# Two attention layers with feed-forwards on one core: biases in a held column of the tokens, parts straight from PSUM, exponentials by head

## The chip, the cores and the metric

One core of a Trainium2 chip. The metric is the device time of one execution in microseconds (us). The kernel before takes 317.99 us (median of three runs, 317.55 to 318.81).

## What is computed

The input is 2048 tokens of 256 channels (two sequences of 1024) and a context of 77 tokens of 192 channels per sequence. Four residual steps follow one another; the tokens are normalised ahead of each:

```
x = x + attention16(layernorm(x), context) # 16 heads of 16 channels, softmax over 77 keys
x = x + y, y = layernorm(n + relu(n @ w1 + b1) @ w2 + b2) * gamma + beta, n = layernorm(x)
x = x + attention1(layernorm(layernorm(x)), layernorm(context)) # one head of 256 channels
x = x + layernorm(x) @ W[e(t)].T + b[e(t)] # e(t): one of 8 matrices, by the position t alone
```

`e(t)` is the argmax over 8 of the product of a fixed position table with the signs of a small matrix. All data is float32. The operands of the products for q, the scores, w1 and w2 are split into a high part (rounded to the engine's fast float32 form, `F32R`) and a low part (the rest), and three products are added: high x high, high x low, low x high.

## The kernel before, in words

The tokens are cut into NG = 8 groups of 256, in two batches of four groups. A group is two halves `i` of 128 tokens, one token per partition. Each group goes through four stages, named by letters: A (first attention), B (feed-forward; Y is the normalisation of its output), C (second attention), D (the routed product). All five engines run their own list of steps, written out by hand at the end of `tensor`, `vector`, `scalar`, `gpsimd` and `sync`. Each engine works through its list strictly in order, waits on semaphores inside the steps, and so interleaves groups and stages as the lists say. Nothing else sets the order.

The steps that the text speaks of, for group g:

- `stats(K, g)` on VectorE: L598, L601, L604, mean and variance. `rs(K, g)` on GpSimd (L1220): the variance to the power of -0.5. `apply(K, g)`: a 2-element product on VectorE (L609, minus mean times that power), then half 0 of the tokens is normalised on VectorE (L619) and half 1 on ScalarE (L1029).
- `tA`, `tB`, `tC`, `tD` on TensorE (L327): transposes into a PSUM bank. `hi` on ScalarE (L1037) copies the bank as the high part XTH; `lo` on VectorE (L625) subtracts and leaves the low part XTL.
- `q(g)`: 12 matmuls (L256); `qh` on ScalarE (L1046) and `ql` on VectorE (L632) add b_q and split, in two instructions each.
- A tile of scores is (g, i, a), a the half of the heads: 32 tiles of 128 tokens x 8 heads x 77 keys. `sc` (L365) writes it into one of the two score banks S. `smax` (L649) takes the maximum by head. For a = 0 it is negated (L652), and ScalarE takes eight exponentials by head with accumulated sums (L1060). For a = 1 VectorE subtracts the maxima into SBUF (L654), one exponential runs over the whole tile (L1064), and VectorE sums (L662). The function `by_head` says which.
- `tE` transposes the exponentials (L375, L377), `rr` and `et` on ScalarE bring reciprocal sums and exponentials into place (L1072, L1083, L1084), `pv`, `o`, `wo`, `x1` finish the attention.
- `w1(g, j)`, j = 0..3: 24 matmuls in pairs of 12, into a bank. `hf` on ScalarE (L1094, two instructions) adds b1, takes the ReLU and writes HF (three buffers). `hh` on VectorE (L682), or `hhA` on ScalarE for j = 1 (L1102), rounds to the high part HH. The low part HL comes from `hlP` on GpSimd (L1254), or `hlD` on VectorE for j = 1, 3 of groups 0, 6, 7 (L688). `w2(g, i, h)`: 12 matmuls, h the half of the hidden channels. `b2` and `be` on GpSimd add bias and beta; `y`, `x2` on VectorE end the stage.
- `r_expert`, `r_position`, `r_index`, `r_pairs` on VectorE: the routing (L837 is an instruction of `r_position`), once. `f_*`: the constants of the second attention, once (L249, L471).
- `pc` on ScalarE (L1139), `pr` on TensorE (L460), `pa` on VectorE (L752): the routed product, eight pairs of 128-token pieces for each batch. Where a piece starts is read from EV by `value_load` the first time. `put` on GpSimd (L1282) stores.

A PSUM bank is held until a step has read it:

```
P = hold(("sc", g, i, a), ("S", k), ("ex", n + 1) if by_head(i, a) else ("sub", n // 2 + 1))
P = hold(("w1", g, j), ("B", p), ("hf", 4 * g + j + 1))
```

Of the kernel before, what the change touches and what calls it, by code (L numbers as in the profile page):

```python
# [15 lines left out]
NK = 77  # L16
CW = 124
NP = 15
# [31 lines left out]
def f(ap):  # L50
    return ap.bitcast(F32)
# [10 lines left out]
def by_head(i, a):  # L62
    return a == 0


def late(g):
    return g in (0, 6, 7)


def hl_on_dve(g, j):  # L70
    return late(g) and j in (1, 3)


def hh_on_act(j):
    return j == 1


def upto(rule, *at):

    g, j = at  # L80
    return sum(bool(rule(a, b)) for a in range(g + 1) for b in range(4) if (a, b) <= (g, j))


def program(nc, A, out):
    with ExitStack() as ctx:
# [12 lines left out]
        nhalf = sb("nhalf", [128, 2])  # L98
        X = sb("X", [128, NG, 2, 256])
# [5 lines left out]
        cols = sb("cols", [128, 22])  # L105
        COLS = dict(b_q=0, b_k=2, bk1=4, bq1=6, bv1=8, g1=10, be1=12, b1=14)
# [18 lines left out]
        HF = sb("HF", [128, 3, 2, 256])  # L125
# [3 lines left out]
        SM = sb("SM", [128, 11, 2, 11])  # L129
# [47 lines left out]

        def raw(n, parts=128, w=512):
            return RAW[0:parts, n % 2, 0:w]
# [40 lines left out]
        def hl_here(w, g, j):  # L220
            if hl_on_dve(g, j):
                w.wait_ge(s["hlD"], upto(hl_on_dve, g, j))
            else:
                w.wait_ge(s["hlP"], 4 * g + j + 1 - upto(hl_on_dve, g, j))

        def hh_here(w, g, j):
            if hh_on_act(j):
                w.wait_ge(s["hhA"], g + 1)
            else:
                w.wait_ge(s["hh"], 3 * g + (j + 1 if j < 1 else j))  # L230

# [3 lines left out]
        def tensor(e):  # L235
# [42 lines left out]
            def vrep(b, p):  # L278
# [3 lines left out]
                w.wait_ge(s["d"], 6)  # L282
# [35 lines left out]
            def turn(K, g, p, signal, until):  # L318
# [4 lines left out]
                w.wait_ge(s["bi" + K], g + 1)  # L323
                P = hold(("t" + K, g), ("B", p), until)
# [87 lines left out]
            def w2(g, i, h, p):  # L412
# [996 lines left out]
```

## Time and profile before

| | |
|---|---|
| median of 3 runs | 317.99 us (317.55 to 318.81) |
| the profiled execution, first to last instruction | 314.0 us |
| its own time beside the span | not listed apart; the median stands 4.0 us over the span |
| mean granted TensorE clock | 0.93 of full speed |
| busy: TensorE matmuls, VectorE | 267.9 us, 254.8 us |
| busy: ScalarE, GpSimd | 181.7 us, 157.3 us |
| DMA moved | 15.3 MB, mean 49 GB/s |

Busy time is the time in which an engine has an instruction under way. The matmuls are pipelined, so a busy TensorE need not be at its peak. Instructions of one engine overlap a little, so the distance between their starts can be less than the duration of one.

### The profile page before, as it was taken

How to read it: one execution, taken by the hardware profiler on the slowest of the kernel's cores; microseconds unless marked ns; L12 is line 12 of the kernel's file. 1: busy time of each engine (PE TensorE's matmuls, PEld its weight loads, DVE VectorE, ACT ScalarE, POOL GpSimd, SP SyncE). 2: the span in 40 equal slices, each digit the busy share in tenths (PEclk: the TensorE clock that was granted, in tenths of full speed). 3: DMA queues.
4: the chain of work that ended last, by engine and by line, in shares of the span. 5: the costliest groups of instructions: out<-in, count | busy, mean ns of one | idle time of the engine just before them, and what ended most of it. 6: DMA issues, size and time to landing. Idle time of an engine off the chain costs nothing.

```text
span 314.0 us, 6283 instructions
## 1 busy us (share of the span) xinstructions
PE 267.9 (85%) x2080; PEld 232.0 (74%) x2080; DVE 254.8 (81%) x664; ACT 181.7 (58%) x606; POOL 157.3 (50%) x157
## 2 busy tenths in 40 slices
PE   2954958977999998999999989999989999878960
PEld 2743937763999698689789959988878988666850
DVE  2998998972889999998997789899899986875640
ACT  2468628526368857478695857775754471454510
POOL 2253640275225878821652263268766653164854
PEclk9995596995999999999999999999999999997995
DMA  6922010240000372100001000011110000000222
GB/s 177 336 72 77 8 42 25 67 142 27 3 0 3 115 222 51 29 24 2 2 0 35 2 0 2 33 52 51 37 36 0 2 0 1 3 0 34 87 78 73
DMA packets 8797, 15.32 MB, mean 49 GB/s; under 512 B 1270, under 2 KB 6813, under 8 KB 8509
## 3 DMA queue, kind: packets, MB, share of 16 engines
q1 hardware_dynamic: 6845, 9.68, 9.2%
q0 software_dynamic: 1920, 5.25, 5.9%
q8 instruction: 17, 0.28, 0.4%
q14 instruction: 15, 0.12, 0.1%
HBM read 11.77 MB, written 3.15 MB: 48 GB/s over the span
## 4 chain that ended last, share of the span: by engine, by line
PE 37%; DVE 29%; issue 15%; POOL 12%; ACT 3%; DVEq 1%; DMA 1%; POOLq 0%; SPq 0%; ACTq 0%
PE PB L256 16%; PE PB L249 7%; PE PB L460 5%; DVE SM L598 3%; POOL SM L1220 3%; DVE SX L649 3%; DVE SM L609 3%; PE S L365 3%; PE S L377 2%; POOL out_x L1282 2%; DVE WD L837 2%; PE PB L327 2%; POOL RAW L1275 2%; DVE XN L701 2%; POOL HL L1254 2%
## 5 line engine op out<-in xcount | busy, mean ns | idle before, releaser
L1220 POOL TENSOR_TENSOR SM<-SM,nhalf 128x2 f32<-128x2 f32 x40 | 29.4, 737 | 98.4 <-DVE SM L604 97.9
L1060 ACT ACTIVATE E<-S,SX 128x77 f32<-128x77 f32 x128 | 39.5, 340 | 16.8 <-DVE SX L652 16.6
L256 PE MATMUL PB<-XTH,W1H 128*128 128x256 f32 x128 | 38.3, 299 | 3.9 <-issue 2.2
L1254 POOL TENSOR_TENSOR HL<-HF,HH 128x512 fp32r<-128x512 f32 x26 | 34.5, 1335 | 13.6 <-DVE HH L682 12.0
L1094 ACT ACTIVATE HF<-PB,cols 128x256 f32<-128x256 f32 x64 | 26.8, 473 | 20.9 <-PE PB L256 20.6
L256 PE MATMUL PB<-W2H,HH 128*128 128x256 f32 x128 | 37.9, 296 | 1.1 <-DVE HL L688 1.1
L256 PE MATMUL PB<-XTH,W1L 128*128 128x256 f32 x128 | 36.4, 284 | 0.0
L256 PE MATMUL PB<-XTL,W1H 128*128 128x256 f32 x128 | 36.4, 284 | 0.0
L256 PE MATMUL PB<-W2H,HL 128*128 128x256 f32 x128 | 35.8, 280 | 0.0
L256 PE MATMUL PB<-W2L,HH 128*128 128x256 f32 x128 | 35.8, 279 | 0.0
L460 PE MATMUL PB<-WD,XP 128*128 x120 | 29.9, 402 | 0.8 <-issue 0.8
L256 PEld LDWEIGHTS PB<-XTH,W1H 128*128 128x128 f32 x128 | 24.5, 192 | 6.2 <-issue 3.9
L649 DVE TENSOR_REDUCE SX<-S 128x8 f32<-128x616 f32 x32 | 25.2, 788 | 3.9 <-PE S L365 3.8
L1060 ACT ACTIVATION_READ_ACCUMULATOR E<-S,SX 128x1 f32 x128 | 28.4, 222 | 0.0
L460 PEld LDWEIGHTS PB<-WD,XP 128*128 128x128 f32 x120 | 23.1, 200 | 5.7 <-issue 2.1
L327 PE MATMUL PB<-ident,XN 128*128 128x128 f32 x128 | 20.1, 289 | 8.0 <-ACT XN L1029 4.7
L1029 ACT ACTIVATE XN<-X,SM 128x256 f32<-128x256 f32 x32 | 19.0, 601 | 13.2 <-DVE SM L609 12.9
L256 PEld LDWEIGHTS PB<-W2H,HH 128*128 128x128 f32 x128 | 24.2, 189 | 2.7 <-issue 2.6
L752 DVE SCALAR_TENSOR_TENSOR X<-PB,MK,X 128x256 f32 x30 | 14.5, 483 | 13.6 <-DVE X L752 6.8
L598 DVE BATCH_NORM_STATS2 SM<-X 128x6 f32<-128x256 f32 x64 | 23.9, 415 | 1.7 <-DMA X<-in_x 1.5
L256 PEld LDWEIGHTS PB<-XTH,W1L 128*128 128x128 f32 x128 | 24.7, 193 | 0.0
L256 PEld LDWEIGHTS PB<-XTL,W1H 128*128 128x128 f32 x128 | 24.6, 192 | 0.0
(188 smaller groups left out, 778.3 us busy)
## 6 DMA issues: line engine op xcount, KB each, us to landing
RAW<-in_w SPq DMA_DIRECT2D x4, 512.0 KB, 5.0
WD<-in_WD SPq DMA_DIRECT2D x2, 1024.0 KB
X<-in_x SPq DMA_DIRECT2D x4, 256.0 KB, 7.1
x<-X SPq DMA_DIRECT2D x4, 256.0 KB, 2.2
bc<-in_rows SPq DMA_DIRECT2D x1, 768.0 KB, 7.3
RAW<-in_w_q SPq DMA_DIRECT2D x1, 256.0 KB, 4.2
Wo<-in_w_o SPq DMA_DIRECT2D x1, 256.0 KB, 7.8
RAW<-in_WqT SPq DMA_DIRECT2D x1, 256.0 KB
```

Of the source, the lines that this page charges most:

```text
L249: t = e.matmul(dst, a, b, start=j == 0, stop=j == len(pairs) - 1)
L256: t = e.matmul(dst, a, b, start=first and j == 0, stop=last and j == n - 1)
L327: t = e.transpose(P[:, c * 256 + i * 128:c * 256 + (i + 1) * 128], xn[:, i, c * 128:(c + 1) * 128], ident[:, :])
L460: t = e.matmul(P[:, v * 256:(v + 1) * 256], XP[:, r % 2, v, c * 128:(c + 1) * 128], WD[:, c, bass.ds(start[n], 256)], start=c == 0, stop=c ...
L598: step(e.bn_stats(smi(K, g, i, 0, 6), src[:, i, :]))
L649: step(e.tensor_reduce(mx_, sv, AX, ALU.max))
L752: t = e.scalar_tensor_tensor(out=x, in0=P[:, v * 256:(v + 1) * 256], scalar=MK[:, n:n + 1], in1=x, op0=ALU.mult, op1=ALU.add)
L1029: e.activation(dst_of(K, g)[:, 1, :], src_of(K, g)[:, 1, :], ACT.Identity, bias=smi(K, g, 1, 10, 11), scale=smi(K, g, 1, 9, 10)).then_inc( ...
L1060: t = e.activation(Ei[:, h * NK:(h + 1) * NK], P[:, at:at + NK], ACT.Exp, bias=SX[:, i, 2, k:k + 1], accum_out=SX[:, i, 1, k:k + 1])
L1094: t = e.activation(HF[:, n % 3, v, :], P[:, v * 256:(v + 1) * 256], ACT.Relu, bias=col("b1", 2 * j + v))
L1220: e.tensor_tensor(sm(K, g, 9), sm(K, g, 8), nhalf[:, :], ALU.pow).then_inc(s["rs" + K], 1)
L1254: e.tensor_tensor(HL[:, hs, :], HF[:, (4 * g + j) % 3, :, :], f(HH[:, hs, :]), ALU.subtract).then_inc(s["hlP"], 1)
```

## The change

- b_q and b1 become the last row of w_q and w1. The normalised tokens of a group sum to zero over the channels, so channel 255 is given by the others: the step `pivot` on VectorE subtracts the last row of the weights from all others, and column 255 of the normalised tokens is held at one. GpSimd's `one` writes it, `apply` leaves it out for A and B, and GpSimd puts the true value back before the residual (in `b2`). The old last rows are loaded, broadcast to 128 partitions, as WQR and W1R.
- With no bias left, `qh` and `ql` are one instruction each, and the high part HH of the feed-forward is a ReLU straight from PSUM on ScalarE (`hh`). The low part is one VectorE instruction from PSUM (`hl`). HF, `hf`, `hhA`, `hlP` and `hlD` are gone; `w2` waits for the two j of its own half. The bank of w1 is held until `hl`.
- All 32 tiles of exponentials are taken by head with sums. The maximum is negated in its own instruction (`negate=True`).
- The product of minus mean and the power moves from VectorE to GpSimd as two 2-element products.
- The routing's values are loaded in one block per engine (`starts`), early.
- All five lists are in a new order.

```
-                P = hold(("w1", g, j), ("B", p), ("hf", 4 * g + j + 1))
+                P = hold(("w1", g, j), ("B", p), ("hl", 4 * g + j + 1))
...
-                for j in range(4):
-                    hh_here(w, g, j)
-                    hl_here(w, g, j)
+                w.wait_ge(s["hh"], 4 * g + 2 * h + 2)
+                w.wait_ge(s["hl"], 4 * g + 2 * h + 2)
...
+            def starts():
+                w.wait_ge(s["route2"], 1)
+                load_starts(e, 0, 7 * 256, start)
...
+            def pivot(n):
+                w.wait_ge(s["m_id"], 1)
+                if n == 0:
+                    step(e.tensor_scalar(nkeep[:, :], ident[:, 127:128].to_broadcast([128, 2]), 1.0, None, ALU.subtract))
+                    settle()
+                w.wait_ge(s[("wq", "w1a", "w1b")[n]], 16)
+                w.wait_ge(s[("wqr", "w1r", "w1r")[n]], 16)
+                W, R, by = ((RAW[:, 0, 0:512], WQR, None), (RAW[:, 1, 0:1024], W1R, -1.0), (RAW[:, 0, 0:1024], W1R, keep))[n]
+                if n == 0:
+                    step(e.scalar_tensor_tensor(out=W[:, 0:256], in0=R, scalar=-1.0, in1=W[:, 0:256], op0=ALU.mult, op1=ALU.add))
+                    W, by = W[:, 256:512], keep
+                e.scalar_tensor_tensor(out=W, in0=R, scalar=by, in1=W, op0=ALU.mult, op1=ALU.add).then_inc(s["wfix"], 1)
...
+                e.tensor_reduce(two(SX[:, i, 0, 8 * a:8 * a + 8]), sv, AX, ALU.max, negate=True).then_inc(s["mx"], 1)
...
+            def hl(g, j):
+                w.wait_ge(s["hh"], 4 * g + j + 1)
                 hs = slice(2 * j, 2 * j + 2)
-                e.tensor_tensor(HL[:, hs, :], HF[:, (4 * g + j) % 3, :, :], f(HH[:, hs, :]),
-                                ALU.subtract).then_inc(s["hlD"], 1)
+                e.scalar_tensor_tensor(out=HL[:, hs, :], in0=two(bank("w1", g, j)[:, :]), scalar=0.0, in1=f(HH[:, hs, :]),
+                                       op0=ALU.max, op1=ALU.subtract).then_inc(s["hl"], 1)
...
+                for h in range(8):
+                    at = h // 4 * 512 + h % 4 * NK
+                    k = 8 * a + h
+                    t = e.activation(E[:, i, a, h * NK:(h + 1) * NK], P[:, at:at + NK], ACT.Exp,
+                                     bias=SX[:, i, 0, k:k + 1], accum_out=SX[:, i, 1, k:k + 1])
                 t.then_inc(s["ex"], 1)
...
+                e.activation(HH[:, 2 * j:2 * j + 2, :], two(bank("w1", g, j)[:, :]), ACT.Relu).then_inc(s["hh"], 1)
...
+                if K != "Y":
+                    e.tensor_tensor(sm(K, g, 11), sm(K, g, 6), minus[:, :], ALU.mult).then_inc(s["nm"], 1)
...
+                    e.tensor_tensor(sm(K, g, 10), sm(K, g, 11), sm(K, g, 9), ALU.mult).then_inc(s["mr" + K], 1)
+                if K == "B":
+                    e.tensor_tensor(sm(K, g, 8), X[:, g, :, LAST], sm(K, g, 9), ALU.mult).then_inc(s["xm"], 1)
```

What stands ahead of w1(0, 0) on TensorE before (PB are banks; WD and RAW rows are the second attention's constants and the routing's permutation):

```order
L375 MATMUL S<-ident,RR 128x128
L377 MATMUL S<-ident,E 124x128 x5
L249 MATMUL PB<-WD,RAW 128x154 x4
L315 MATMUL PB<-WD 128x16 x8
L249 MATMUL PB<-WD,RAW 128x154 x4
L327 MATMUL PB<-ident,XN 128x128 x4
L365 MATMUL S<-KBH,XTH 128x308 x2
...
L256 MATMUL PB<-XTH,W1H 128x256
```

And in the changed kernel (L359 is tE, L371 pv, L347 sc, L309 a transpose, L227 wo):

```order
L371 MATMUL PB<-ET,VB 32x256 x8
L206 TENSOR_LOAD EV
L206 ISA x30
L309 MATMUL PB<-ident,XN 128x128 x4
L227 MATMUL PB<-Wo,RT 128x256 x4
L347 MATMUL S<-KBH,XTH 128x308 x2
L347 MATMUL S<-KBL,XTH 128x308 x2
L347 MATMUL S<-KBH,XTL 128x308 x2
...
L309 MATMUL PB<-ident,XN 128x128 x4
L234 MATMUL PB<-XTH,W1H 128x256
```

The constants are gone from this place. The block of register loads stands ahead of tB(0), and the scores of group 2 and the transpose of group 4 ahead of w1.

ScalarE around the high part of B(0) before (L1083 and L1084 are et, L1037 the high part, L1094 hf):

```order
L1144 ACTIVATE WD<-PB 96x308
L1064 ACTIVATE E<-E 128x616
L1083 ACTIVATE RT<-S 128x128
L1084 ACTIVATE ET<-S 124x5x128
L1029 ACTIVATE XN<-X,SM 128x256
L1072 ACTIVATE RR<-SX 128x128
L1037 ACTIVATE XTH<-PB 128x512
```

And in the changed kernel (L1013 is the high part, L1030 the exponentials, L1058 hh):

```order
L1050 ACTIVATE RT<-S 128x128
L1051 ACTIVATE ET<-S 124x5x128
L206 TENSOR_LOAD EV
L206 ISA x30
L1030 ACTIVATE E,SX<-S,SX 128x77 x16
L1013 ACTIVATE XTH<-PB 128x512
L1005 ACTIVATE XN<-X,SM 128x255
...
L1030 ACTIVATE E,SX<-S,SX 128x77 x8
L1058 ACTIVATE HH<-PB 128x512 x2
```

The block and two tiles of group 2 by head now stand ahead of the high part of B(0).

VectorE at the first routed additions before (L750 are the loads and their checks, L752 the additions):

```order
L750 TENSOR_LOAD EV
L750 ISA x2
L752 ISA
L752 SCALAR_TENSOR_TENSOR X<-PB,MK,X 128x256
...
L598 BN_STATS SM<-X 128x6 x2
L601 BN_AGGR SM<-SM 128x2 x2
L604 TENSOR_SCALAR SM<-SM 128x2
```

And in the changed kernel (L724 the additions, L671 and L677 are x2 of group 7):

```order
L671 SCALAR_TENSOR_TENSOR XN<-XN,SM,bc 128x256 x2
L677 SCALAR_TENSOR_TENSOR X<-XN,SM,X 128x256 x2
L612 TENSOR_SCALAR XN<-X,SM 128x256
L724 ISA
L724 SCALAR_TENSOR_TENSOR X<-PB,MK,X 128x256
```

The additions have no load ahead of them, and the first of them stands behind x2 of the last group, where before two pairs stood ahead of y(7).

## Rows read from the trace of the kernel before

**Rows 1.** The page, part 1: busy time, share of the span, instructions.
```profile
PE 267.9 (85%) x2080; PEld 232.0 (74%) x2080; DVE 254.8 (81%) x664; ACT 181.7 (58%) x606; POOL 157.3 (50%) x157
```

**Rows 2.** Windows: stretch, length, busy of each engine, clock, DMA share, GB/s.
```profile
0.00:83.00 83.00, 58.59 (x437) 48.58 (x438) 62.68 (x174) 43.71 (x148) 32.01 (x38) 0.81 0.29 92
83.00:266.00 183.00, 175.92 (x1488) 156.61 (x1488) 165.79 (x419) 121.94 (x416) 101.85 (x95) 1.00 0.10 30
266.00:304.00 38.00, 33.40 (x159) 26.77 (x157) 25.84 (x71) 16.03 (x42) 18.58 (x19) 0.96 0.10 36
```

**Rows 3.** Waits of TensorE from 0 to 83 us: total, times, longest.
```profile
PE PB L249 <- DMA WKV<-in_w_k: 5.9, 1, 5.9
PE S L365 <- DVE E L654: 4.5, 1, 4.5
```

**Rows 4.** Groups of VectorE: count, busy us, mean ns, idle before.
```profile
L609 DVE SCALAR_TENSOR_TENSOR SM<-SM 128x2 f32<-128x2 f32 x32 | 15.1, 472 | 2.8 <-POOL SM L1220 2.7
L654 DVE TENSOR_TENSOR E<-S,SX 128x616 f32<-128x616 f32 x16 | 12.8, 799 | 0.6
L682 DVE CAST HH<-HF 128x512 fp32r<-128x512 f32 x24 | 12.5, 524 | 8.2 <-ACT HF L1094 7.3 <-issue 0.7
L662 DVE TENSOR_REDUCE SX<-E 128x8 f32<-128x616 f32 x16 | 12.4, 778 | 0.5 <-ACT E L1064 0.5
L625 DVE TENSOR_TENSOR XTL<-PB,XTH 128x512 fp32r<-128x512 f32 x16 | 10.8, 681 | 2.1 <-ACT XTH L1037 1.9
L688 DVE TENSOR_TENSOR HL<-HF,HH 128x512 fp32r<-128x512 f32 x6 | 7.1, 1200 | 0.1
L652 DVE TENSOR_SCALAR SX<-SX 128x8 f32<-128x8 f32 x16 | 5.7, 353 | 0.5
```

**Rows 5.** Groups of GpSimd, same columns.
```profile
L1254 POOL TENSOR_TENSOR HL<-HF,HH 128x512 fp32r<-128x512 f32 x26 | 34.5, 1335 | 13.6 <-DVE HH L682 12.0 <-ACT HH L1102 1.5
L1220 POOL TENSOR_TENSOR SM<-SM,nhalf 128x2 f32<-128x2 f32 x40 | 29.4, 737 | 98.4 <-DVE SM L604 97.9
L1209 POOL TENSOR_TENSOR W1L<-RAW,W1H 128x1024 fp32r<-128x1024 f32 x2 | 4.8, 2390 | 1.2 <-ACT W1H L1003 1.2
```

**Rows 6.** Timeline of VectorE at 18 and 36 us: start, duration.
```profile
17.98 2.00 DVE L609 SCALAR_TENSOR_TENSOR SM<-SM 128x2 f32<-128x2 f32 x1
36.38 6.24 DVE L837 TENSOR_TENSOR WD<-WD 128x64 f32<-128x64 f32 x1
```

**Rows 7.** Timeline of ScalarE: the first of eight heads, and what follows the eighth.
```profile
21.25 0.33 ACT L1060 ACTIVATE E<-S,SX 128x77 f32<-128x77 f32 x1 [3.05 <-DVE SX L652]
...
23.66 0.63 ACT L1029 ACTIVATE XN<-X,SM 128x256 f32<-128x256 f32 x1
```

**Rows 8.** Groups of ScalarE, columns as in rows 4.
```profile
L1094 ACT ACTIVATE HF<-PB,cols 128x256 f32<-128x256 f32 x64 | 26.8, 473 | 20.9 <-PE PB L256 20.6 <-POOL HL L1254 0.2
L1037 ACT ACTIVATE XTH<-PB 128x512 fp32r<-128x512 f32 x16 | 9.6, 606 | 12.8 <-PE PB L327 12.8
```

**Rows 9.** Timeline of TensorE: start of w1(0,0) and of w2(0,0,0).
```profile
63.95 0.36 PE L256 MATMUL PB<-XTH,W1H 128*128 128x256 f32 x1
82.62 0.36 PE L256 MATMUL PB<-W2H,HH 128*128 128x256 f32 x1
```

**Rows 10.** Window up to the high part of B(0), columns as in rows 2.
```profile
5.90:61.40 55.50, 41.34 (x306) 35.03 (x306) 49.35 (x127) 34.97 (x117) 18.83 (x18) 0.78 0.28 92
```

**Rows 11.** Waits of ScalarE in the same window.
```profile
ACT E L1060 <- DVE SX L652: 9.7, 3, 5.5
ACT XTH L1046 <- PE PB L256: 5.4, 2, 4.1
```

**Rows 12.** Timeline of VectorE: additions with a load, and without.
```profile
262.61 0.48 DVE L752 SCALAR_TENSOR_TENSOR X<-PB,MK,X 128x256 f32 x1 [0.76 <-DVE X L752]
297.50 1.11 DVE L752 SCALAR_TENSOR_TENSOR X<-PB,MK,X 128x256 f32 x2 [0.62 <-PE PB L460]
```

**Rows 13.** Timeline of GpSimd: the last of the stores.
```profile
309.45 0.96 POOL L1282 DMA_INDIRECT out_x<-X,SI  x1 [0.30 <-issue]
```

More of the change, by code:

```diff
@@ L59, in flat2 @@
     return T.rearrange("p a b -> p (a b)")
[L62 to L81, printed above, removed]
 def program(nc, A, out):
@@ L176, in program @@
         QB = WD[:, 1, 768:1024].rearrange("p (c t) -> p c t", c=2)
+        LAST = 255
+        W1R = X[:, 6:8, :, :].rearrange("p g i n -> p (g i n)")
+        WQR = X[:, 5, 0, :]
+        keep = nkeep[:, 0:1]
         def raw(n, parts=128, w=512):
@@ L218, in x2_here, with load_starts @@
             w.wait_ge(s["x2"], 2 * g + 2)
[L220 to L230, printed above, removed]
+        def load_starts(e, row, most, at):
+            values = nc.values_load_multi_w_load_instructions(EV[0:1, row, 0:NP], engines=[e.engine],
+                                                              min_val=0, max_val=most)[1]
+            for n in range(NP):
+                at[n] = values[n]
         place = {}
@@ L323, in turn @@
                 w.wait_ge(s["bi" + K], g + 1)
+                if K == "A":
+                    w.wait_ge(s["one"], 1)
+                elif K == "B":
+                    w.wait_ge(s["one"], max(g, 1) + 1)
                 P = hold(("t" + K, g), ("B", p), until)
@@ L456, in pr @@
                     n = 2 * r + v
-                    if n not in start:
-                        start[n] = e.value_load(EV[0:1, 0, n:n + 1], min_val=0, max_val=7 * 256)
                     for c in range(2):
@@ L628, in ql @@
             def ql(g):
-                w.wait_ge(s["qh"], 2 * g + 2)
-                P = bank("q", g)
-                for m in range(2):
-                    e.scalar_tensor_tensor(out=XTL[:, 1 + g % 2, m, :], in0=P[:, m * 256:(m + 1) * 256],
-                                           scalar=col("b_q", m), in1=f(XTH[:, 1 + g % 2, m, :]),
-                                           op0=ALU.add, op1=ALU.subtract).then_inc(s["ql"], 1)
-            def scores(g, i, a):
+                w.wait_ge(s["qh"], g + 1)
@@ L658, in ssum @@
-            def ssum(g, i, a):
-                n, sv, mx_, hs = scores(g, i, a)
-                w.wait_ge(s["ex"], n + 1)
-                if not by_head(i, a):
-                    step(e.tensor_reduce(SX[:, i, 1, hs], E[:, i, a, 0:8 * NK].rearrange("p (h k) -> p h k", h=8),
-                                         AX, ALU.add))
-                    settle()
+                    w.wait_ge(s["ex"], n - 3)
+                e.tensor_reduce(two(SX[:, i, 0, 8 * a:8 * a + 8]), sv, AX, ALU.max, negate=True).then_inc(s["mx"], 1)
@@ L737, in vector, with starts @@
             begin = {}
+            def starts():
+                w.wait_ge(s["route2"], 1)
+                load_starts(e, 1, 7 * 256, begin)
             def pa(b, r):
@@ L748, in pa @@
                         settle()
-                    if n not in begin:
-                        begin[n] = e.value_load(EV[0:1, 1, n:n + 1], min_val=0, max_val=7 * 256)
                     x = tokens[:, bass.ds(begin[n], 256)]
@@ L1128, in scalar, with starts @@
             start = {}
+            def starts():
+                w.wait_ge(s["route2"], 1)
+                load_starts(e, 2, 7 * 128, start)
             def pc(b, r):
                 w.wait_ge(s["xtd"], 4 * b + min(r, 3) + 1)
-                w.wait_ge(s["route2"], 1)
                 if 8 * b + r > 1:
```

370 lines of the change are left out of this document (171 added, 199 removed), and 2 rows, old and new, of the table SIGNALS.

## The prediction

> **What bounds the kernel now.** I read the page first: TensorE (PE) is busy 85% of the span, VectorE (DVE) 81%, ScalarE (ACT) 58%, GpSimd (POOL) 50% [rows 1]. Shares over a whole span hide stages, so next the windows [rows 2]. From 83 to 266 us PE is busy 175.9 of 183: it is the bound there, and DVE with 165.8 is close behind. In the first 83 us PE is busy 58.6, at a mean granted clock of 0.81, that is partly at the lower level (1.2 GHz, the other is 2.4): 24.4 us idle. From 266 to 304 it misses 4.6 us. Then 10 us hold only stores. Its waits in the front [rows 3] begin with the first weights (DMA, 5.9); a score bank that only DVE's subtraction empties costs 4.5. The rest are tokens and low parts, paced by DVE and ACT. Little can be won in the middle: no PE work is removed by the change. So the question is when PE gets into its dense stretch, and what the tail costs. The sum is made against the profiled span of 314.0 us. The median of the runs, 317.99, is 4.0 above it, and I add that at the end.
>
> **DVE and POOL, part by part.** DVE loses 16 subtractions (0.80 each, 12.8 us), 16 sums (12.4), 16 negations (5.7), 32 small products (15.1), 24 casts (12.5), 6 low parts (7.1) and, since two half instructions become one, some 2 us of low parts of q [rows 4]. It gains 32 low parts of the feed-forward from PSUM. Their nearest row is the subtraction with one PSUM operand of the same size, 0.68 us [rows 4]; bounds are 0.68 and the 1.20 of the variant with both operands in SBUF. I take 0.68: 21.8 us. Four weight corrections on DVE are new. They cover 2560 columns, and by 0.68 for 512 [rows 4] cost 3.4 us, up to 6.0 by the 1.20 of the SBUF variant. Net DVE -40, so 255 becomes about 215. POOL loses 34.5 us of those low parts and gains about 88 tiny instructions. The trace has no 2-element product there. The rows of 512 and 1024 columns, 1.34 and 2.39, give 2.39 - 2 x 1.05 = about 0.25 us of fixed cost, an estimate; the power of two elements, 0.74, is the upper bound [rows 5]. I take 0.25, +22 us, with 65 as the end of the range: POOL 157 to 145. Two products now sit between the power and ACT's half of each normalisation, 0.5 us, but not behind DVE's queue.
>
> A row shows what tiny instructions really pay: the 128x2 product on DVE takes 2.00 us at 18 us, where POOL splits w1 (2.39 for 1024 columns), and a 64-element product stands 6.24 us while POOL goes through three instructions in a row [rows 5, 6]. The Trainium skill (GPSIMD Engine Reference, Specifications) says that GpSimd shares its SBUF interfaces with VectorE, with contention for instructions in a 2-port mode or with two SBUF inputs. By this rule, the trace agrees, the new low parts (one input in PSUM) are not held. By the same rule the corrections of w1, two SBUF inputs of 1024 columns, can be held by a POOL product; the sum would then have up to 2 x 2.4 us more on DVE in the front. Without the rule, the 6.24 us row alone is the reason why I leave 5 us of holding in the front's range.
>
> **ACT.** The exponentials of a tile by head start 0.30 us apart: eight from 21.25 to 23.66, 2.41 us a tile [rows 7], though one lasts 0.33, with the reading of its sum behind it: they overlap. Sixteen tiles change to this from one batched exponential of 616 columns, which I put at the 0.61 of a 512-column copy [rows 8]: +28.8 us. The feed-forward needs 32 instructions of 0.61 (the PSUM copy of that size) where 64 of 0.47 stood, and 8 rounding copies of 0.61 [rows 8]: -15 by their durations, -12 with the overlap. One copy of q's high part for two: -2. ACT goes from 182 to about 197: no bound of the whole, but in the front it is a chain.
>
> **The front, 0 to 83 us.** My marker is where the second feed-forward product (w2) of group 0 begins: 82.62 us now; the first (w1) began at 63.95 [rows 9]. The new order puts one more score tile, two more transposed tiles, q of groups 3 and 4 and the transposes of groups 3 and 4 ahead of it, and the second attention's constants behind it. By the distances of the same steps' starts in the timeline I estimate 5.9 us more and 5.0 us less done by PE at the marker, 0.9 net. ACT's way to the high part of B(0), which releases w1: now it ends at 61.5 us, with ACT busy 35.0 of the 55.5 us from 5.9 to 61.4 [rows 10]. Changed: six more tiles by head (+14.4), four batched away (-2.4), two more copies of transposed exponentials (+1.7), the rest about +0.5, the table load now earlier (-1.3): 47.9. The first 5.4 us of waiting for q stay [rows 11]. The 9.7 us behind the negations mostly go: 5.5 of them were the routing's 6.24 [rows 6, 11], and now scores are reduced with the sign in one instruction, with routing between tiles. I keep 2. New is the block of register loads: one load and 30 checks on PE, ACT and DVE. One load with its checks costs DVE 1.25 - 0.63 = 0.62 us now [rows 12]; 15 cost at most 9.3; in one block with a single load I take 2.5. The correction of wq delays the first q by about 1 us. So 5.9 + 47.9 + 5.4 + 2 + 2.5 + 1 = 64.7 us. From there w2 follows by two exponential tiles (4.8 us), five short ACT steps of 0.5 each, w1's four blocks of 1.4 partly beside them, and a low part: about 10.5 us. Now 21.1 pass, since the routing's pairs stand between on DVE and the constants on PE; the new order has both elsewhere. Marker at 75.2: 7.4 earlier, with 0.9 more done: **-8**. Bounds: all PE waits of the front go except the first 5.9 of DMA, about -13; or ACT keeps its 20.5 us idle (55.5 less 35.0) and the block costs 9.3: +11. For the -13: of 24.4 us idle the 5.9 of DMA and about 5 up to the first q stay.
>
> **The middle.** PE's 7.1 idle us are the ceiling of a gain. DVE gets 40 us lighter, POOL leaves the feed-forward, but a score bank is held 2.41 us instead of a 0.80 us subtraction, and the second attention's constants now come in here. **-2**, between -6 and +4.
>
> **The tail.** DVE's routed additions into the tokens pay 1.25 us each with a load ahead, 0.63 without [rows 12]. All 15 loads leave the stage where the last group's chain (residual, statistics, transposes, routed product) waits on DVE. PE idles 4.6 us from 266 to 304 [rows 2]; it now has all 16 routed products behind the last w2 (two stood ahead of it), more to cover the chain with: **-4**, between -5 and 0. The end stays: the last eight stores, the last at 309.45, with 0.96 + 0.30 us for each, and the landing [rows 13]. They wait for the same additions of the second batch. Sum -14: span 300, time 304.
>
> **Rivals.** (1) ACT starves the front: each of the ten tiles ahead of B(0) takes 2.41 us on ACT and the banks wait for it. For: ACT's busy share in the front rises from 35 to 48 of 55 us. Against: its idle there was another engine's lateness. With the old idle of 20.5 and 9.3 for the block, the high part of B(0) ends at 83.6, 19 later than forecast, and the marker is at 94.1: front +10.6, tail -4, middle 0: span 320.6, time 325. It decides once that copy ends after 79 us: at 73 the front gains nothing, and 6 us more eat the middle and the tail. (2) Everything dense: front -13, middle -5, tail -5: time 295. For: no engine is over 75% but PE. Against: ACT is a chain in the front, and the middle's idle us are short and spread. (3) POOL's tiny products cost as much as its power, 0.74: POOL 188 us, 1 us more on each application; in the last chains of C and D some 6 us: time 310. (4) The change moves waits without removing them: the second attention's constants, late and off the old idle time, take back what the front gave: 317.
>
> **How the numbers follow.** Forecast 304 +- 6: 0.54. Rival 1: 0.18. Rival 2: 0.13. Rival 3: 0.09. Rival 4: 0.06. The range takes the forecast, rivals 3 and 4 and the edge of each other one: 294 to 320. A measurement of this kernel tells about 0.5%, 1.6 us, from no change. Faster: 0.54 + 0.13 + 0.09 = 0.76; same 0.06; slower 0.18.
>
> **What would show it.** DVE at 215 us busy, ACT at 197, POOL at 145; exponentials 128x77 twice as many at an unchanged 0.30 spacing; ACT's first feed-forward step at about 67 us, w2 at about 75; PE without 1 us gaps after 90; DVE's routed additions 0.63 apart; store spacing 1.26. The forecast is wrong if the B(0) high copy on ACT ends after 73 us, if the register block stands over 5 us on PE, or if PE's busy share from the marker to the stores falls under 95%.

## The result, and the profile after

The changed kernel takes **297.82 us** (median of 4 runs, 296.64 to 298.7), the kernel before beside it 317.77 (315.01 to 318.81): ratio 0.942, 95% interval 0.936 to 0.949. It is faster by 20 us, where 14 were forecast. The median lies in the range (294 to 320) and 0.2 us below the forecast's own 298 to 310. On another chip a second set gave 296.08 against 313.46, ratio 0.940 (0.934 to 0.946). Some executions take 1.5% longer and more than the fastest of the same kernel; ratios and their intervals leave those out, medians and ranges do not.

The page of the changed kernel, part 1 [rows 1]:

```profile
span 294.8 us, 6416 instructions
PE 260.7 (88%) x2080; PEld 230.1 (78%) x2080; DVE 212.1 (72%) x584; ACT 195.3 (66%) x798; POOL 139.1 (47%) x218
```

DVE lost 43 us, POOL 18, ACT gained 14: forecast were 215, 145 and 197. Next its windows: up to the first w2, to the end of the last w2, and the rest. Columns as in [rows 2].

```profile
0.00:79.10 79.10, 58.28 (x449) 48.40 (x449) 59.73 (x173) 58.21 (x256) 39.23 (x59) 0.87 0.29 94
79.10:247.40 168.30, 165.88 (x1449) 151.49 (x1447) 123.40 (x331) 118.18 (x492) 72.14 (x123) 1.00 0.13 38
247.40:294.80 47.40, 36.51 (x188) 30.21 (x186) 28.97 (x81) 18.91 (x51) 27.77 (x37) 0.93 0.13 45
```

The kernel before, cut at the same two steps:

```profile
0.00:82.60 82.60, 58.19 (x434) 48.18 (x435) 62.31 (x173) 43.71 (x148) 32.01 (x38) 0.81 0.29 93
82.60:266.20 183.60, 176.52 (x1493) 157.21 (x1493) 166.15 (x420) 121.94 (x416) 101.85 (x95) 1.00 0.10 30
266.20:314.00 47.80, 33.20 (x158) 26.57 (x155) 26.32 (x72) 16.03 (x42) 23.46 (x24) 0.88 0.13 45
```

The three lengths differ by -3.5, -15.3 and -0.4 us, together the 19.2 of the spans. But the stages don't hold the same work. To set them side by side I took, for each kind of matmul, the distance from its start to the next start where nothing holds it (the lower quartile of all such distances of that kind). Summed, that is PE's work: 210.5 us before and 211.2 after, so no work was saved. What is left of the time between starts is loss: 86.6 and 67.0 us.

| stage | length | work | loss |
|---|---|---|---|
| front, to the first w2 | 82.6 -> 79.1 | 36.0 -> 37.8 | 40.7 -> 35.4 |
| middle, to the end of the last w2 | 183.6 -> 168.3 | 146.2 -> 139.3 | 37.8 -> 29.0 |
| tail and stores | 47.8 -> 47.4 | 28.4 -> 34.0 | 8.1 -> 2.5 |

(The loss doesn't count the 5.9 us before the first matmul and the 10 to 11 from the last matmul to the end, which are nearly equal; the rows add up to within about 1 us.) So 5.3 us came from the front, 8.8 from the middle, 5.6 from the tail. The tail is as long as before, though two routed pairs moved into it. The front's 5.3 is the weakest of the three: another execution of the old front, in run 10, ended at 76.9 with a loss of 35.4 by the same count, no more than the changed kernel's.

The rows that answer to those of before: groups of DVE, ACT and POOL [rows 4, 5, 7, 8].

```profile
L658 DVE SCALAR_TENSOR_TENSOR HL<-PB,HH 128x512 fp32r<-128x512 f32 x32 | 21.6, 685 | 5.5 <-ACT HH L1058 4.6
L1058 ACT ACTIVATE HH<-PB 128x512 fp32r<-128x512 f32 x32 | 19.3, 628 | 11.9 <-PE PB L234 11.8
L1030 ACT ACTIVATE E<-S,SX 128x77 f32<-128x77 f32 x256 | 79.0, 364 | 14.1 <-DVE SX L635 8.0
L1179 POOL TENSOR_TENSOR SM<-SM,nhalf 128x2 f32<-128x2 f32 x40 | 29.6, 741 | 85.6 <-DVE SM L598 84.8
L1181 POOL TENSOR_TENSOR SM<-SM,minus 128x2 f32<-128x2 f32 x32 | 6.8, 213 | 0.0
```

The new low parts take 0.68 us, as the subtraction with one PSUM operand did [rows 4], not the 1.20 with both in SBUF. A product of two elements on GpSimd takes 0.21, the power of two elements 0.74.

Timelines of the three engines about the block of register loads: start, duration, idle before. The first row writes EV, which the loads read.

```profile
57.88 0.18 DVE L873 CAST EV<-WD 1x48 int32<-1x48 f32 x1
...
64.61 1.09 PE L309 MATMUL PB<-ident,XN 128*128 128x128 f32 x4 [5.53 <-issue]
63.18 0.33 ACT L1030 ACTIVATE E<-S,SX 128x77 f32<-128x77 f32 x1 [6.02 <-issue]
...
67.99 0.68 ACT L1013 ACTIVATE XTH<-PB 128x512 fp32r<-128x512 f32 x1
69.16 0.69 DVE L653 TENSOR_TENSOR X<-PB,X 128x512 f32<-128x512 f32 x1 [7.24 <-PE PB L227]
```

Each of PE, ACT and DVE stands for 5.5 to 7.2 us about that block; ScalarE's first 0.9 is a wait for EV, and DVE's last 2.9 a wait for wo. The second row of ScalarE is the high part of B(0). The block's own parts on ScalarE: count, duration in ns (least, median, most), first and last start:

```profile
L206 ACTq FUSED_REGOPS  x15: 147/147/167, 59.8 to 62.9; - x15
L206 ACTq TENSOR_LOAD <-EV x1: 1648/1648/1648, 58.1 to 58.1; - x1
```

The one load of 15 values takes 1.65 us; the checks, two for each value, then follow one another for 3.4 us. And the additions of the tail [rows 12], one timeline row of VectorE in the changed kernel:

```profile
278.73 1.11 DVE L724 SCALAR_TENSOR_TENSOR X<-PB,MK,X 128x256 f32 x2 [0.24 <-DVE X L724]
```

Two additions in 1.11 us, with 0.24 ahead of the pair: no load stands between them any more.

### The profile page after: what moved, and what is told of

Read it like the earlier page. It is cut to its first block, busy times and chain, and to the rows that moved or that the text cites. A ratio compares the mean times of both kernels' runs of the same rounds, so it can differ in the third digit from the quotient of the medians.

```text
span 294.8 us, 6416 instructions
## 1 busy us (share of the span) xinstructions
PE 260.7 (88%) x2080; PEld 230.1 (78%) x2080; DVE 212.1 (72%) x584; ACT 195.3 (66%) x798; POOL 139.1 (47%) x218
## 3 DMA queue, kind: packets, MB, share of 16 engines
q1 hardware_dynamic: 7133, 10.33, 10.4%
## 4 chain that ended last, share of the span: by engine, by line
PE 63%; DVE 13%; issue 7%; POOL 7%; ACT 7%; DMA 1%; POOLq 0%; SPq 0%; DVEq 0%; ACTq 0%
PE PB L234 29%; PE PB L227 12%; PE PB L371 5%; PE S L359 5%; POOL out_x L1251 5%; PE S L347 5%; PE PB L309 4%; ACT E L1030 3%; DVE SM L592 2%; DMA WKV<-in_w_k 1%; PE PB L274 1%; DVE X L724 1%; PE S L357 1%; DVE HL L658 1%; POOL X L1239 1%
## 5 line engine op out<-in xcount | busy, mean ns | idle before, releaser
L1030 ACT ACTIVATE E<-S,SX 128x77 f32<-128x77 f32 x256 | 79.0, 364 | 14.1 <-DVE SX L635 8.0
L1030 ACT ACTIVATION_READ_ACCUMULATOR E<-S,SX 128x1 f32 x256 | 62.4, 246 | 0.0
L234 PE MATMUL PB<-XTH,W1H 128*128 128x256 f32 x128 | 37.7, 294 | 1.1 <-DVE XN L665 0.5
L635 DVE TENSOR_REDUCE SX<-S 128x8 f32<-128x616 f32 x32 | 24.6, 791 | 5.5 <-PE S L347 5.4
L442 PE MATMUL PB<-WD,XP 128*128 x120 | 28.2, 383 | 0.2
L1058 ACT ACTIVATE HH<-PB 128x512 fp32r<-128x512 f32 x32 | 19.3, 628 | 11.9 <-PE PB L234 11.8
L1005 ACT ACTIVATE XN<-X,SM 128x255 f32<-128x255 f32 (+1 forms) x32 | 19.5, 613 | 9.6 <-POOL SM L1185 9.3
L658 DVE SCALAR_TENSOR_TENSOR HL<-PB,HH 128x512 fp32r<-128x512 f32 x32 | 21.6, 685 | 5.5 <-ACT HH L1058 4.6
L309 PE MATMUL PB<-ident,XN 128*128 128x128 f32 x128 | 20.1, 285 | 5.8 <-issue 5.5
L442 PEld LDWEIGHTS PB<-WD,XP 128*128 128x128 f32 x120 | 22.1, 190 | 3.9 <-issue 0.8
L234 PEld LDWEIGHTS PB<-W2L,HH 128*128 128x128 f32 x128 | 24.2, 189 | 0.1
```

What stands on the lines that cost most here:

```text
L234: t = e.matmul(dst, a, b, start=first and j == 0, stop=last and j == n - 1)
L309: t = e.transpose(P[:, c * 256 + i * 128:c * 256 + (i + 1) * 128], xn[:, i, c * 128:(c + 1) * 128], ident[:, :])
L442: t = e.matmul(P[:, v * 256:(v + 1) * 256], XP[:, r % 2, v, c * 128:(c + 1) * 128], WD[:, c, bass.ds(start[n], 256)], start=c == 0, stop=c ...
L635: e.tensor_reduce(two(SX[:, i, 0, 8 * a:8 * a + 8]), sv, AX, ALU.max, negate=True).then_inc(s["mx"], 1)
L658: e.scalar_tensor_tensor(out=HL[:, hs, :], in0=two(bank("w1", g, j)[:, :]), scalar=0.0, in1=f(HH[:, hs, :]), op0=ALU.max, op1=ALU.subtract ...
L1005: e.activation(dst_of(K, g)[:, 1, 0:n], src_of(K, g)[:, 1, 0:n], ACT.Identity, bias=smi(K, g, 1, 10, 11), scale=smi(K, g, 1, 9, 10)).then_ ...
```

## Experiments

Times are medians; a ratio is against the kernel before on the same chip. "From the changed kernel" and "from the kernel before" say which was edited.

**1. Loads late again** (from the changed kernel). All three blocks out, loads back at the routed pairs:

```diff
-pv(1, 1); starts(); tB(0, 0)
+pv(1, 1); tB(0, 0)
...
 def pr(b, r, p):
...
+    if n not in start:
+        start[n] = e.value_load(EV[0:1, 0, n:n + 1], min_val=0, max_val=7 * 256)
```

The same in pc on ScalarE and in pa on VectorE.

> The changed kernel with its register loads late again, one by one at the routed pairs on TensorE, ScalarE and VectorE, as before; no block. Theory 1 (the block pays for itself): the front begins 5 us earlier (the block stands 5.5 to 6 us on three engines at once, which wait for each other anyway), the tail gives back more: 15 x 0.62 us on VectorE where the last chain waits for it. Time 300 to 303, against 297.8 of the changed kernel. Theory 2 (the tail's loads were hidden, since PE has 16 routed products and VectorE is idle a quarter of the time there): only the front's gain shows, 292 to 294.

Measured: 304.18 us, ratio 0.958 (0.952 to 0.964). Windows with the same cuts:

```profile
0.00:77.30 77.30, 58.17 (x449) 49.59 (x449) 59.68 (x173) 58.48 (x256) 38.83 (x59) 0.87 0.31 96
77.30:246.10 168.80, 166.24 (x1451) 151.76 (x1449) 123.25 (x332) 118.12 (x492) 72.09 (x123) 1.00 0.13 38
246.10:302.90 56.80, 37.32 (x186) 29.43 (x184) 30.54 (x81) 19.81 (x51) 27.50 (x37) 0.93 0.11 38
```

The front ends 1.8 us earlier (the theory said 5), the middle is the same within 0.5, the tail is 9.4 us longer. Its timeline of VectorE shows the loads at the old price, and PE now waits for the additions behind them (its group of routed products sat idle 3.9 us, 0.2 in the changed kernel):

```profile
262.11 0.48 DVE L729 SCALAR_TENSOR_TENSOR X<-PB,MK,X 128x256 f32 x1 [0.75 <-DVE X L729]
...
269.06 0.48 DVE L729 SCALAR_TENSOR_TENSOR X<-PB,MK,X 128x256 f32 x1 [0.75 <-DVE X L729]
```

Theory 1 holds, 1.2 us above its range: the early loads are worth 6.4 us net by the medians (4.9 by the ratios).

**2. The block on VectorE alone** (from the changed kernel): edits of run 1 on TensorE and ScalarE only.

> The changed kernel with the block on VectorE alone; TensorE and ScalarE load late, one by one. Theory 1 (the three blocks run side by side and the slowest sets the front): VectorE's own 7.2 us stay in the way of the tokens of B(0), so the gain is small, 0 to 2 us: 296 to 298. Theory 2 (ScalarE's block is the path, since exponentials and the high part of B(0) follow it): 4 to 5 us less, 293. The late loads on TensorE and ScalarE cost about nothing in the tail by both.

Measured: 297.64 us, ratio 0.937 (0.932 to 0.943), the same as the changed kernel. The first w2 begins at 78.8 (79.1). That looks as if the other two blocks had cost nothing. But the steps ahead of the blocks, which the edit leaves alone, came 2.4 us later in this execution. Its rows of VectorE:

```profile
60.28 0.18 DVE L876 CAST EV<-WD 1x48 int32<-1x48 f32 x1
...
68.86 0.69 DVE L656 TENSOR_TENSOR X<-PB,X 128x512 f32<-128x512 f32 x1 [3.42 <-PE PB L227]
```

From the start of the cast that writes EV to the first w2 it is 18.5 us here. In the profiles with three blocks it is 21.2, 21.5 and 21.6 (the changed kernel, runs 11 and 9), in those with none 17.6, 17.7 and 16.5 (runs 1, 3 and 12). So the blocks of TensorE and ScalarE cost the front some 3 us: with them, VectorE's x1 (69.16) waited 2.9 us beyond its own block for wo, which stood behind TensorE's. VectorE's block alone costs 1 to 2: its last check is at 68.7 here, and x1 and the low part that w1 waits for follow at once. The tail is 49.4 us instead of 47.4: late loads on TensorE and ScalarE are not free. The time is the one of theory 1, but its picture of three blocks side by side does not hold: what the two gave back was taken again by the tail and, in the profiled execution, by the late start.

**3. VectorE's loads one by one over the middle** (from the changed kernel), TensorE and ScalarE late:

```diff
+def start_of(n):
+    begin[n] = e.value_load(EV[0:1, 1, n:n + 1], min_val=0, max_val=7 * 256)
...
-smax(3, 1, 1)
+smax(3, 1, 1); start_of(0)
...
-smax(7, 0, 1)
+smax(7, 0, 1); start_of(14)
```

> The changed kernel without a block: TensorE and ScalarE load late, VectorE loads its 15 values one by one, one behind each of 15 maxima of groups 3 to 7. If a single load costs about the 0.62 us of the tail before, VectorE pays 9.3 us more in the middle, where it is busy 123 of 168 us. Theory 1 (VectorE's delays reach TensorE in the middle): each load is a small stall, some 3 to 5 us come back and the time is 295 to 298. Theory 2 (VectorE has slack there now): the front's 5 us are won, the tail keeps its gain: 292 to 293.

Measured: 295.61 us, ratio 0.932 (0.927 to 0.938). Windows:

```profile
0.00:76.30 76.30, 58.40 (x448) 47.67 (x449) 60.45 (x173) 58.37 (x256) 39.10 (x59) 0.89 0.30 97
76.30:244.90 168.60, 165.99 (x1449) 151.52 (x1448) 123.25 (x331) 118.13 (x492) 71.82 (x123) 1.00 0.13 38
244.90:294.40 49.50, 37.05 (x188) 29.71 (x187) 29.28 (x81) 19.48 (x51) 27.73 (x37) 0.94 0.12 43
```

The front gains 2.8 us (3.6 from the cast that writes EV), the middle takes the 15 loads without a trace (168.6 against 168.3), the tail pays 2.1 for TensorE's and ScalarE's late loads. The time lies in theory 1's range, but its mechanism, stalls in the middle, did not come; theory 2's slack did, and its 292 to 293 was missed by the front's smaller gain and the tail.

**4. The changed kernel's work in the order of before.** The lists of all engines are those of before, with the new steps put where the old ones stood; loads late. For group 0, ScalarE first and then VectorE:

```diff
-hf(0, 0); hf(0, 1); apply("A", 3); hhA(0, 1); hf(0, 2)
+hh(0, 0); hh(0, 1); apply("A", 3); hh(0, 2)
...
-hh(0, 0); hh(0, 2); o(1); f_kv(1); hlD(0, 1); hh(0, 3)
+hl(0, 0); hl(0, 1); hl(0, 2); o(1); f_kv(1); hl(0, 3)
```

> All the work of the changed kernel in the order of the kernel before (its lists on each engine, with the casts and low parts of the feed-forward mapped onto the new copies, and the loads late). Theory 1 (lighter VectorE and GpSimd bring the middle's gain, and the front's as well): within 3 us of the changed work in the new order with late loads. Theory 2 (the order brings the gain: constants out of the front, routing between tiles, all routed products behind the last w2): 308 to 318, since the second attention's constants and the routing stand where they stood. My own guess lies between: 306 to 310, with the front lost and the middle kept.

Measured: **348.20 us**, ratio 1.098 (1.089 to 1.106). Against run 1, which has the same work, the old order costs 44 us; against the kernel before, the new work costs 30. No theory reached that far. Waits of TensorE (total, times, longest):

```profile
PE S L347 <- ACT E L1037: 11.7, 3, 8.8
PE PB L234 <- DVE HL L663: 6.6, 4, 3.2
PE PB L309 <- ACT XN L1012: 6.2, 2, 5.5
...
PE S L357 <- ACT E L1037: 5.6, 2, 3.5
PE PB L371 <- DVE HL L663: 4.2, 2, 2.5
```

17.3 us are waits for exponentials (in the changed kernel 1.8 + 1.9), 15.5 for low parts (with two smaller groups, of 2.9 and 1.8). VectorE is busy 62% here: it is light, and it doesn't help.

**5. The exponentials by head alone** (from the kernel before, order as before):

```diff
 def by_head(i, a):
-    return a == 0
+    return True
...
-("ex", n + 1) if by_head(i, a) else ("sub", n // 2 + 1)
+("ex", n + 1)
...
-step(e.tensor_reduce(mx_, sv, AX, ALU.max))
+e.tensor_reduce(mx_, sv, AX, ALU.max, negate=True).then_inc(s["neg"], 1)
```

> The kernel before with one part of the change alone: all 32 exponential tiles by head with their sums, negated maxima in one instruction (no subtractions, no sums and no negations on VectorE: 16 x 0.80 + 12.4 + 5.7 = 31 us off, ScalarE 29 us more). Order as before. Theory 1 (VectorE's load bounds the small stalls of the middle): faster, by 3 to 8 us: 310 to 315. Theory 2 (what counts is that order and durations fit: a bank now stays held through 2.41 us on ScalarE where 0.80 us of VectorE released it, and the order was made for the latter): slower, 320 to 335; the run of all the new work in the old order, 348, speaks for this.

Measured: 328.25 us, ratio 1.050 (1.042 to 1.059): slower, though VectorE fell from 254.8 to 226.6 us. This is theory 2. TensorE waits 15.2 + 5.8 us for exponentials. The middle is 197.7 us:

```profile
82.70:280.40 197.70, 182.34 (x1492) 162.21 (x1493) 143.13 (x388) 142.90 (x596) 100.64 (x95) 0.97 0.10 28
```

**6. Old order, half the tiles batched again** (run 4 with VectorE's subtraction, one exponential and VectorE's sum for the tiles of a=1):

```diff
+if a:
...
+    e.tensor_tensor(LESS[:, i, :].rearrange("p (u h k) -> p u h k", u=2, h=4), sv,
+                    two(SX[:, i, 0, 8:16]).unsqueeze(3).to_broadcast([128, 2, 4, NK]),
+                    ALU.add).then_inc(s["sub"], 1)
...
-P = hold(("sc", g, i, a), ("S", k), ("ex", n + 1))
+P = hold(("sc", g, i, a), ("S", k), ("sub", n // 2 + 1) if a else ("ex", n + 1))
```

> The run of the new work in the old order, with one part undone: the 16 exponential tiles of a=1 are batched again (VectorE subtracts in 0.80 us and releases the bank). The held column, the feed-forward from PSUM, the products on GpSimd stay. Theory A (in the old order the score banks, held through 2.41 us on ScalarE, cost the 30 us; the run of before with exponentials by head alone lost 15): back to 315 to 325, and TensorE's wait of 17.3 us for exponentials shrinks to under 8. Theory B (the feed-forward's bank, now held until the low part, and its place in VectorE's list cost it): 335 or more.

Measured: 325.90 us, ratio 1.041 (1.035 to 1.047). By the ratios 5.7% of the 9.8% come back, some 18 us: theory A, in its larger part. TensorE's waits for exponentials are gone (5.8 us are now for one subtraction). What is left looks like theory B: TensorE now waits longest for low parts, 20.6 us in all. No run took that part away by itself.

```profile
PE PB L235 <- DVE HL L675: 13.5, 7, 2.7
...
PE PB L446 <- DVE HL L675: 2.9, 1, 2.9
...
PE PB L372 <- DVE HL L675: 2.5, 1, 2.5
```

**7. The same tiles batched in the new order** (from the changed kernel, edit of run 6).

> The changed kernel with the 16 exponential tiles of a=1 batched again: maxima subtracted on VectorE (0.80 us, releases the bank) into a buffer of its own, one exponential of 616 columns, sums on VectorE (0.78). VectorE 212 to 237, ScalarE 195 to about 166. Theory 1 (VectorE's relief is what counts): 3 to 6 us slower, 301 to 304. Theory 3 (ScalarE's chain of 2.41 us a tile is what holds the front's banks now): the front gets shorter by part of 6 x 1.8 us, the time falls to 292 to 296. Theory 2 (order): within 2 us of 297.8.

Measured: 304.91 us, ratio 0.978 (0.970 to 0.987). In the new order the same edit costs 8 us (296.49 is run 9 on the same chip, and the spans are 302.8 and 294.8), where in the old it gave about 18. The first w2 is at 83.6 (4.5 later), the middle 3.5 longer. Theory 3 falls: ScalarE is 26 us lighter (169.0), VectorE 21 heavier (233.5), and the front is longer. Theory 2 falls too; theory 1 holds, 0.9 us over its range.

**8. 31 us of idle copies on VectorE** (from the changed kernel):

```diff
+def fill():
+    e.tensor_copy(FILL[:, 1 + filled[0] % 2, :], FILL[:, 0, :]).then_inc(s["fl"], 1)
```

It is called behind each of the 32 maxima and of the 32 low parts.

> The changed kernel with 64 more instructions on VectorE, that nobody waits for: a copy of 512 columns in SBUF behind each of the 32 maxima and each of the 32 low parts of the feed-forward (output unchanged). By the 0.52 us of the casts before, 33 us more: VectorE 212 to 245, near its 255 before. Theory 1 (the middle's gain of about 8.6 us came from VectorE's relief): most of it goes, plus some of the front: 305 to 312. Theory 2 (the order gave it, VectorE's load doesn't matter under 80%): 298 to 300.

Measured: 304.30 us, ratio 0.973 (0.964 to 0.982). The 64 copies took 0.485 us each, 31.0 together, but they overlap their neighbours: VectorE is busy 234.4, 22.3 more. Against run 9 on the same chip the time is 7.8 us longer. Windows of the front and the middle:

```profile
0.00:81.90 81.90, 59.86 (x449) 51.26 (x449) 63.83 (x187) 58.77 (x256) 39.36 (x59) 0.83 0.27 90
81.90:255.40 173.50, 167.67 (x1449) 151.60 (x1446) 141.51 (x382) 118.68 (x492) 73.81 (x123) 1.00 0.13 37
```

18.1 us more of VectorE in the middle make it 5.2 us longer, at a busy share of 82%. Only 3.4 of these show as idle time of PE; its "busy" time rose by 1.8 for the same work, and the loss between starts rose from 29.0 to 34.5. Theory 1 holds, though 304.30 lies 0.7 us below its range. Run 7 agrees: there 15.3 us more of VectorE (138.7 against 123.4) go with 3.5 us more in the middle, with a lighter ScalarE.

**9. Idle products on GpSimd** (from the changed kernel): two more of two elements between the power and the minus-mean product, for each of 32 normalisations.

```diff
+e.tensor_tensor(idle[:, 0, :], minus[:, :], minus[:, :], ALU.mult).then_inc(s["nn"], 1)
+e.tensor_tensor(idle[:, 1, :], minus[:, :], minus[:, :], ALU.mult).then_inc(s["nn"], 1)
```

> The changed kernel with two more idle products of two elements on GpSimd between the power and the minus-mean product, for each of 32 normalisations (output unchanged): 0.21 us each by the row of after, 13.6 us more on GpSimd, 0.4 to 0.5 us more ahead of ScalarE's half. If the tokens' normalisation is on the path of the middle, as TensorE's waits for the tokens say, up to 32 x 0.4 = 13 us could come, but most are covered: theory 1 gives 299 to 302, with the front's six normalisations and the last ones paying. Theory 2 (GpSimd has slack everywhere): within 1 us, 297 to 299.

Measured: 296.49 us, ratio 0.949 (0.941 to 0.958). Busy time of GpSimd rose to 147.0, the span is 295.2 against 294.8, the middle 167.9 against 168.3. The changed kernel was not run on this chip, and the ratios of the two (0.949 and 0.942) leave room for some 2 us; their intervals overlap. So the lengths of the stages are the better evidence that GpSimd has slack in the middle and the tail (47.4 us in both); the front ended at 80.0, as in run 11 (80.1).

**10. VectorE's loads spread, alone** (from the kernel before; start_of as in run 3):

```diff
-smax(3, 1, 1); apply("A", 5)
+smax(3, 1, 1); start_of(0); apply("A", 5)
```

> The kernel before with one part alone: VectorE's 15 register loads taken out of the tail and put one by one behind 15 maxima of groups 3 to 7; all else as before. The run with late loads showed the tail 9.7 us longer in the new order. Theory 1 (the tail of before pays the same 15 x 0.62): tail 5 to 9 us shorter, the middle, where VectorE is busy 166 of 184, up to 3 us longer: net 2 to 9 us faster. Theory 2 (before, TensorE's other work hid the loads in part, 14 pairs instead of 16 in the tail): 0 to 3 us faster.

Measured: 310.65 us, ratio 0.988 (0.984 to 0.992), 1.2% faster. The tail is 2.4 us shorter (45.4), the middle 1.9 longer (185.5): nearly nothing net in the stages that the edit touches, and nearer to theory 2. The profile's front is 5.7 us shorter, where nothing was edited:

```profile
0.00:76.90 76.90, 55.90 (x434) 47.05 (x435) 64.25 (x171) 43.47 (x148) 32.16 (x38) 0.84 0.31 99
```

The two timelines of TensorE part inside w1(0). The kernel before waits twice there, and from 70 to 77 us its granted clock is 0.51, the lower level, so that the 32 products of pv take 3.59 us; in the run above they take 1.93. The kernel before:

```profile
69.26 0.39 PE L256 MATMUL PB<-XTH,W1H 128*128 128x256 f32 x1 [2.19 <-issue]
...
73.61 3.59 PE L389 MATMUL PB<-ET,VB 124*32 124x256 f32 x32 [2.16 <-ACT HF L1094]
```

The 12 runs lie in two groups, 308.6 to 310.7 (7 runs) and 313.4 to 313.8 (5), and the profiled run was one of the lower group. That this stretch divides them was not tried. So part of the front's 5.3 us, perhaps all of it, may be how the one profiled execution of the kernel before fell out: against the 76.9 here, the changed kernel's fronts of 79.1 and 80.1 gain nothing. The 17 runs of the kernel before on this chip spread over 309.1 to 316.4 as well.

**11 and 12. The changed kernel and run 3 once more**, on one chip.

> The changed kernel once more, unchanged, beside the next one on the same chip: ratio 0.942 as in its first runs, within 0.007.

> The changed kernel with VectorE's loads spread over the middle and no blocks (as in the earlier run, with one wait on the routing added, met long before). It was 0.932 of before where the changed kernel was 0.942. If the block's 2 to 3 us in the front are real, it is again 2 us or more faster than the run beside it; if that was the spread of the measurement, within 1 us.

Measured: 296.08 us (293.56 to 300.11), ratio 0.940; 294.08 us (291.67 to 296.58), ratio 0.937 (0.932 to 0.942). The changed kernel came out as expected. The spread loads were 2.2 us faster by the medians of the first set (3.1 by the ratios) and 2.0 by these, but by these ratios only 1.1 us, between the two marks of the expectation, and the intervals overlap each time: likely, not settled. The first w2 began at 80.1 and 75.9. Run 12 is the fastest version run here.

## Why the prediction was right, and where it was not

- **What was right**: the direction, the range, and the busy times; not the stages. The stage terms were -8, -2 and -4, together -14; the lengths changed by -3.5, -15.3 and -0.4, together -19.2. Counted by the loss, which leaves out work that only changed its stage, they are -5.3, -8.8 and -5.6: the front 2.7 us worse than forecast, the middle 6.8 and the tail 1.6 better. The front's miss covers part of the middle's. That the median stands so near the forecast, and not some 3 us lower at the edge of the range, is luck.
- **DVE, ACT, POOL loads**: 212, 195, 139 against 215, 197, 145. Right. DVE's listed terms add up to -42.4, not the -40 that was written; it measured -42.7. The 0.25 us for a tiny product, from the difference of two long rows, measured 0.21; rival 3 (0.74 each) is out, and run 9 shows little or no cost for even more of them. The 0.61 for a batched exponential was a wrong stand-in: the kernel before has it at 0.73, as run 7 has, so the +28.8 us for ScalarE were 1.9 too many. The low part at 0.68 held, and so did the unchanged 0.30 between heads: 16 heads with the reading of their sums filled 63.18 to 67.99. The holding that the Trainium skill's rule allowed for the corrections of w1 (GPSIMD Engine Reference, Specifications) did not come: they took 1.17 and 1.28 us, and the four corrections 3.4 together, as forecast. That neither was held doesn't test the rule: they ran from 23.8 to 26.2 us, and GpSimd had nothing under way for the 6.2 us up to 28.56.
- **Front, -8 forecast, -3.5 on the clock and -5.3 with the work**: the sum's form was right, one term was not. The high part of B(0) was to end at 64.7 and ended at 68.67; the first w2 was to begin at 75.2 and began at 79.1, so the whole error stands ahead of that copy. The failed term is "in one block with a single load I take 2.5". ScalarE stood 6.0 us, 0.9 of it for EV and 5.0 in the block. The load was cheap, 1.65 us for 15 values; the 30 checks, 3.4 us, are what the term left nearly out. A value cost 0.34 us against 0.62 for a load of its own: less than half off, not three quarters. The sum's other terms were off too, but nearly cancelled: ScalarE waited 2.9 us for q where 5.4 were kept, 0.9 for the maxima where 2 were kept, 2.1 for the correction of wq where 1 was, and 4.7 for GpSimd's products ahead of its normalisations, which were not in the sum. My mark for a wrong forecast, over 5 us on PE, was passed (5.53), and the block did cost the front: run 3, without the block in the front, has its first w2 2.8 us earlier, 3.6 counted from the cast that writes EV. Whether the front gained at all over the kernel before stays open (run 10).
- **Middle, -2 forecast, -8.8 measured**: the step that failed is "PE's 7.1 idle us are the ceiling of a gain". The work that the order moves out of the middle (6.9 us, two routed pairs above all) was not in the term, and idle time is not the ceiling. The middle's loss between starts was 37.8 us, five times what the window shows as not busy, since the ends of matmuls are modelled and short delays count as busy. Of the gain, 4.7 us came out of idle time (7.1 to 2.4) and the rest out of time that counted as busy (10.6 less, for 6.9 less work). That VectorE's 43 us less is a cause, in the new order, is shown by run 8: 18.1 us put back into the middle cost 5.2, that is 0.29 for one. By that slope the 43 us less in the middle would be worth some 12, an estimate that takes the slope as constant beyond what was tried, and more than the 8.8 found; the rest of the sum, with the opposite sign, was not taken apart.
- **Order and work together**: what the prediction treated as separate (work by its durations, the order by where steps moved) is not. The new work in the old order is 30 us slower than the kernel before, and by head alone 15 slower; batching half the tiles again gives back about 18 in the old order and costs 8 in the new. TensorE's waits say where: 17.3 and 21.0 us for exponentials in the old order (runs 4 and 5), 3.7 in the new. The likely reading is that a score bank held through 2.41 us of ScalarE needs other products between, which the new order supplies; no run moved those steps alone. The prediction named this ("a score bank is held 2.41 us instead of a 0.80 us subtraction") and gave it +4 at most; rival 1 priced it only for the front.
- **Tail, -4 forecast, -5.6 in loss, -0.4 in length**: right in size by the loss; the term left out that the two moved pairs also make the tail longer (5.6 us more work). Its reason holds only in part. With late loads the tail is 9.4 us longer (run 1); 2.0 of that are TensorE's and ScalarE's loads (run 2), so VectorE's 15 make up 7.4, near the full 9.3 of 15 at 0.62, once 16 pairs stand there. In the kernel before the same loads were worth only 2.4 (run 10), with two pairs ahead of the last w2; which of its other waits hid them there was not tried. So the early loads seem to pay mainly for the new place of all 16 pairs.
- **Rivals.** 1 (ACT starves the front) did not come: the copy ended at 68.7, not after 79, and in run 7 a lighter ScalarE with a heavier VectorE made the front longer. 2 (everything dense, 295) is nearest in time and wrong in its parts: its front of -13 did not come, its middle of -5 was too small. 4 is out by the time. No run moved the constants alone, so what they cost in the middle isn't known.
- **Smaller marks.** "PE without 1 us gaps after 90" held: the longest wait of the middle from 90 us on is 0.9. The correction of wq was to delay the first q by 1 us; it began at 12.1 against 12.0. ScalarE's first feed-forward step was to come at about 67 and came at 73.9, behind a tile of exponentials, and yet from the high part's end to w2 it took 10.4 us, 10.5 forecast. The last stores are 1.26 apart, as said.
- PE is busy 98.5% from the first w2 to the stores ((165.88 + 36.46) / 205.4), over the 95% named.

## What to carry to other kernels

When work is moved from one engine to another, the order has to be made again for it: with late loads in both, the same new work was 14 us faster than the kernel before in its own order and 30 slower in the old one, and no sum of busy times shows that. Don't take the idle time of a dense stretch as the ceiling of what can be won: compare starts of equal instructions, and test the slope with idle copies on the engine next to the bound. Before you read a marker in one profile against another, check that the steps ahead of the edit came at the same time; if not, count from the last step that the edit leaves alone. Register loads that many additions wait for don't belong in the last chain; one by one, in a stretch where their engine has slack, they were likely 1 to 3 us better than in a block ahead of the first dense stretch.

## What was not expected of the hardware

- A load of 15 values into registers in one go, with its 30 checks, takes 5.0 us on ScalarE, and TensorE stands 5.5 for it; of the 5.0 the load is 1.65 and the checks 3.4. One value at a time, with its checks, it is 0.5 us on VectorE in the tail (0.75 ahead of an addition with a load, 0.24 without); 15 late loads each on TensorE and on ScalarE together lengthen the tail by 2.
- A product of two elements on GpSimd is 0.21 us, a power of the same two elements 0.74: the operation sets it, not the size.
- One and the same front, with the edit only behind it, differed by 5.7 us between two profiled executions, with two waits of 2.2 us and a stretch at the lower clock in the one that the other has not. A single profile of a kernel with such a front is no measure of it to better than that.
